# The value projection in rounded fp32r passes, its result copied in quarters by two engines, and halo columns copied in pairs

## What is computed

```python
xn = layernorm(x)                             # (4, 2048, 256)
proj = xn @ in_proj_w + in_proj_b             # (4, 2048, 768)
v = proj[..., :256]
for i in range(2):
    ctrl = proj[..., (i + 1) * 256:(i + 2) * 256]
    h = implicit_filter(...)                  # a filter as long as the sequence
    v = fft_conv(v, h)                        # causal convolution of 2048
    xc = conv3(ctrl, conv_w[i]) + conv_b[i]   # three taps a channel, same padding
    v = v * (xc * sigmoid(xc @ gate_w[i] + gate_b[i]))
out = x + v @ out_proj_w + out_proj_b + ffn(xn)
# ffn: relu(bitlinear(xn, w_fc) + gate * rank-16 term) ** 2 through bitlinear(., w_proj)
```

## Time and profile before

| | us |
|---|---|
| Median of three runs | 860.69 (860.06 to 862.17) |
| Profiled execution, time | 857.83 |
| Profiled execution, span of its instructions | 856.0 |

### The profile page before, as it was taken

The page is one execution under the profiler, slowest core; times in us unless marked ns, Lnnn a source line. Parts: engine busy times, 40 slices in busy tenths (PEclk is TensorE's granted clock), DMA queues, the critical chain, the costliest instruction groups (busy, mean ns, idle before and its releaser), DMA issues.

```text
span 856.0 us, 25946 instructions
## 1 busy us (share of the span) xinstructions
PE 830.3 (97%) x9920; PEld 693.7 (81%) x9921; DVE 617.5 (72%) x1054; ACT 471.6 (55%) x701; POOL 201.0 (23%) x235
## 2 busy tenths in 40 slices
PE   8799999999999998999999999999999999999997
PEld 3588887888888867788888888888888888888997
DVE  7988899889988884555655565556646666567887
ACT  6967777777777854454444444444444444443221
POOL 4944566456645301010101010000000000000000
PEclk9999999999999999999999999999999999999999
DMA  8853432342233278768777868778887877951895
GB/s 224 247 218 115 160 120 98 116 161 115 98 120 140 92 188 227 157 152 194 173 169 154 202 150 202 145 181 182 192 149 182 181 183 132 219 109 49 226 321 195
DMA packets 90544, 142.03 MB, mean 166 GB/s; under 512 B 12846, under 2 KB 70591, under 8 KB 89471
## 3 DMA queue, kind: packets, MB, share of 16 engines
q1 hardware_dynamic: 72846, 101.80, 49.9%
q0 software_dynamic: 7728, 28.05, 10.2%
q10 hardware_dynamic: 9920, 11.54, 4.1%
HBM read 97.39 MB, written 43.97 MB: 165 GB/s over the span
## 4 chain that ended last, share of the span: by engine, by line
PE 51%; DVE 5%; issue 3%; DMA 1%; DVEq 0%; SPq 0%
PE pp L1401 14%; PE py L1420 14%; PE pf L1370 12%; PE pf L1376 3%; PE py L1457 2%; PE py L1388 2%; DVE pp L1169 2%; DMA lead<-filters 1%; DVE GC L1179 1%; DVE xb L1179 1%; PE pp L465 1%; PE pp L467 1%; PE pp L466 1%; PE pf L465 1%; PE pf L467 1%
## 5 line engine op out<-in xcount | busy, mean ns | idle before, releaser
L1300 ACT ACTIVATE r<-pf,fscale 128x512 f32<-128x512 f32 x128 | 88.0, 688 | 124.2 <-PE pf L1376 124.0
L1420 PEld LDWEIGHTS py<-vwin,lead 64*64 64x64 f32 x5120 | 132.7, 132 | 26.8 <-issue 26.8
L1420 PE MATMUL py<-vwin,lead 64*64 64x128 f32 (+4 forms) x5120 | 146.9, 265 | 2.2 <-issue 1.3
L1305 ACT ACTIVATE r_hi<-r 128x512 fp32r<-128x512 f32 x128 | 80.8, 632 | 122.9 <-DVE r L1184 122.9
L1370 PE MATMUL pf<-tokens,split_a 128*128 (+1 forms) x512 | 139.4, 394 | 0.4 <-issue 0.4
L1401 PE MATMUL pp<-wproj,r_hi 128*128 128x256 f32 x512 | 134.6, 296 | 3.8 <-DVE GC L1179 1.8
L1189 DVE TENSOR_TENSOR r_lo<-r,r_hi 128x512 fp32r<-128x512 f32 x128 | 88.2, 689 | 67.2 <-ACT r_hi L1305 67.1
L1401 PE MATMUL pp<-wproj,r_lo 128*128 128x256 f32 x512 | 126.8, 281 | 0.0
L506 POOL TENSOR_SCALAR lead<-lead,norms 128x256 f32<-128x256 f32 x64 | 118.0, 1854 | 3.8 <-POOL norms L500 3.4
L674 DVE SCALAR_TENSOR_TENSOR xc<-ctrl,taps,xc 128x512 f32<-128x512 f32 x128 | 97.7, 783 | 18.5 <-ACT xc L781 17.7
L1401 PEld LDWEIGHTS pp<-wproj,r_hi 128*128 128x128 f32 x512 | 96.2, 188 | 18.3 <-issue 7.4
(11 more groups left out here) (190 smaller groups left out, 1504.9 us busy)
## 6 DMA issues: line engine op xcount, KB each, us to landing
lead<-filters SPq DMA_DIRECT2D x128, 320.0 KB, 6.3
xnT_hbm<-split_b SPq DMA_DIRECT2D x32, 512.0 KB, 3.3
tokens<-xnT_hbm POOLq DMA_DIRECT2D x30, 512.0 KB, 4.9
lead<-in_attn_x SPq DMA_DIRECT2D x16, 512.0 KB, 4.0
gc_hbm<-xc SPq DMA_DIRECT2D x16, 512.0 KB, 2.6
GC<-gc_hbm SPq DMA_DIRECT2D x32, 256.0 KB, 6.6
out<-GC ACTq DMA_DIRECT2D x15, 512.0 KB, 7.2
GC<-in_attn_x POOLq DMA_DIRECT2D x9, 512.0 KB, 7.6
```

Of the source, the lines that this page charges most:

```text
L1300: act.activation(r[j][:, :], pf[:, j, :], ACT.Relu, scale=fscale[:, m:m + 1]).then_inc(relu_done, 1)
L1305: act.activation(r_hi[j][:, :], r[j][:, :], ACT.Copy).then_inc(r_hi_done, 1)
L1420: last = pe.matmul(py[g % 2][q * BW:(q + 1) * BW, side, l, :, A:NB], tile[rows, q * PAIR + l, j * BW:(j + 1) * BW], vwin[g % 2][rows, q, l ...
```

## The change

- V is computed by `split_mm`: the two parts of x, in tiles of 128 tokens, are the stationary operands, and the two parts of Wv (`Wvs`, split once in step -1) the moving ones, 256 columns at a time. That is 4 tiles x 2 halves of the contraction x 3 passes, 24 matmuls a step. Tokens now lie on the partitions without a division by side, so that a copy has to move rows from one half of the partitions to the other for half of the data.
- The bias isn't added there. V is written by four copies of 64 partitions by 512 elements (`to_V`), two of VectorE and two of ScalarE (`store_V`), each writing every second block. In the mixing stage the window copy of order 0 becomes four operations of 128x128 that add the bias.
- xnT is gone with `next_rows`; `next_low` subtracts from pT in PSUM.
- The first x tile's split lies in `xcs[1]` rather than in xn, and `ranks` of the setup stage in GC1.
- Both control buffers lie in one tile `ctrls`, and in a step with both neighbours one VectorE copy of two columns, with a stride between them, fills both halo columns of a channel group.
- SyncE's first loads for the mixing stage wait for the last V rather than for the last controls.

```diff
@@ setup
-            dve.wait_ge(xnT_done, 1)
-            dve.tensor_tensor(xn[1][:, :, :], xnT[:, :, :], xn[0][:, :, :].bitcast(F32), ALU.subtract).then_inc(xn_split, 1)
+            dve.wait_ge(x0_copied, 1)
+            dve.tensor_tensor(xn[1], x0_rows[:, :, :], xn[0].bitcast(F32), ALU.subtract).then_inc(xn_split, 1)
@@ project_stage
-        ctrl = [sb(f"ctrl{i}", [P, 4, CH + 2]) for i in range(2)]
+        WIDE = CH + 2
+        ctrls = sb("ctrls", [P, 2, 4, WIDE])
+        ctrl = [ctrls[:, i, :, :] for i in range(2)]
+        ctrl_flat = ctrls[:, :, :, :].rearrange("p i c t -> p (i c t)")
+        Wv_sides = Wv[:, :, :].rearrange("p k (h s c) -> p k h s c", h=KT, s=SIDES)
+        Wvs_sides = [Wvs[:, part, :, :].rearrange("p k (s h c) -> p k h s c", s=SIDES, h=KT) for part in range(2)]
+        pn_tiles = pn[:, :, :].rearrange("p (t u) c -> p t (u c)", u=SIDES)
+        def split_rows(s0):
+            return xcs[ORDERS - 1] if s0 == 0 else [part[:, :, :] for part in xn]
+        def to_V(copy, eng, s, s0, parity):
+            k = s0 % 4
+            rows = slice(parity * BW, (parity + 1) * BW)
+            for side in (parity, 1 - parity):
+                last = copy(V[side * BW:(side + 1) * BW, :, bass.ds(batch(eng, s, s0), 1), TB * k + parity:TB * k + TB:SIDES].rearrange("p c n a -> p c (n a)"),
+                            pn_tiles[rows, :, side * SLOTS_V:(side + 1) * SLOTS_V].rearrange("p t c -> p c t"))
+            last.then_inc(v_stored, 1)
@@ SyncE
-                    sp.wait_ge(ctrl_mm, 4 * NCH)
+                    sp.wait_ge(v_mm, NCH)
@@ halo
+                    if front and back and k:
+                        lows, highs = ((near, inner_near), (far, inner_far)) if par == 0 else ((far, inner_far), (near, inner_near))
+                        into, step_in = c * WIDE + lows[0], 4 * WIDE + highs[0] - lows[0]
+                        first, step_out = c * WIDE + lows[1], 4 * WIDE + highs[1] - lows[1]
+                        last = dve.tensor_copy(ctrl_flat[:, into:into + step_in + 1:step_in], ctrl_flat[:, first + step_out:first - 1:-step_out])
+                        last.then_inc(halo_done, 1)
+                        return
@@ next_low
-                    if s0:
-                        dve.wait_ge(xnT_done, s + 2)
-                    dve.tensor_tensor(xn[1][:, :, :], xnT[:, :, :] if s0 else pT[:, :, :], xn[0][:, :, :].bitcast(F32), ALU.subtract).then_inc(xn_split, 1)
+                    dve.tensor_tensor(xn[1][:, :, :], pT[:, :, :], xn[0][:, :, :].bitcast(F32), ALU.subtract).then_inc(xn_split, 1)
@@ VectorE, step -1
+                    dve.wait_ge(wv_ready, 1 + KT)
+                    for k in range(KT):
+                        last = dve.tensor_tensor(Wvs_sides[1][:, k], Wv_sides[:, k], Wvs_sides[0][:, k].bitcast(F32), ALU.subtract)
+                    last.then_inc(wv_ready, 1)
@@ VectorE, V
-                    dve.tensor_tensor(V[:, :, bass.ds(batch(dve, s, s0), 1), TB * k:TB * k + TB].rearrange("p c n a -> p c (n a)"),
-                                      pn[:, :, :].rearrange("p i c -> p c i"),
-                                      bv_row[:, :].unsqueeze(2).broadcast_to([P, SLOTS_V, TB]), ALU.add).then_inc(v_stored, 1)
+                    to_V(dve.tensor_copy, dve, s, s0, 0)
@@ ScalarE
-                def next_rows():
-                    act.wait_ge(v_mm, s + 1)
-                    act.wait_ge(xn_split, s + 1)
-                    act.activation(xnT[:, :, :], pT[:, :, :], ACT.Copy).then_inc(xnT_done, 1)
-
                 if s0 < 0:
+                    for k in range(KT):
+                        act.activation(Wvs_sides[0][:, k], Wv_sides[:, k], ACT.Copy).then_inc(wv_ready, 1)
...
                 high(3)
+                def store_V():
+                    act.wait_ge(v_mm, s + 1)
+                    if s0 == 0:
+                        act.wait_ge(stored, 16 * STORES)
+                    to_V(lambda out, rows: act.activation(out, rows, ACT.Copy), act, s, s0, 1)
+                if front and back:
+                    store_V()
                 if back:
                     sigmoid(0)
                     sigmoid(1)
                 if ahead:
                     act.wait_ge(xT_mm, s + 2)
-                    if s0:
-                        next_rows()
-                    act.wait_ge(xn_split, s + 1)
                     act.wait_ge(xn_saved[0], 16 * s + 16)
                     act.activation(xn[0][:, :, :], pT[:, :, :], ACT.Copy).then_inc(xn_hi_done, 1)
-                    if s0 == 0:
-                        act.wait_ge(xn_split, s + 2)
-                        next_rows()
+                if s0 == 0:
+                    store_V()
@@ TensorE
-                    for i in range(TB):
+                    for i in range(TT):
...
                         for k in range(KT):
-                            for side in range(SIDES):
-                                last = pe.matmul(pn[side * BW:(side + 1) * BW, i, :].rearrange("p (h c) -> p h c", h=KT),
-                                                 xnT[:, k, ts], Wv_sides[:, k, :, side, :], start=(k == 0), stop=(k == KT - 1))
+                            last = split_mm(pe, pn_tiles[:, i, :], (x_hi[:, k, ts], x_lo[:, k, ts]),
+                                            (Wvs[:, 0, k, :], Wvs[:, 1, k, :]), k == 0, k == KT - 1)
@@ mix_stage, ScalarE window
+                if order:
+                    act.activation(vwin[g % 2][:, :, :, :, :].rearrange("p b l n a -> p b l (n a)"),
+                                   Vs[:, :, bass.ds(channels(m, g), PAIR), :], ACT.Copy).then_inc(window_done, 1)
+                    return
+                for b in range(SIDES):
+                    for l in range(PAIR):
+                        channel = bass.ds(channels(m, g) + l, 1)
+                        last = act.activation(vwin[g % 2][:, b, l, :, :].rearrange("p n a -> p (n a)"),
+                                              Vs[:, b, channel, :].rearrange("p c x -> p (c x)"), ACT.Identity, bias=bv_slots[:, b, channel])
+                last.then_inc(window_done, 1)
```

More of the change, by code:

```diff
@@ L50, with setup_stage @@
 HALF = PARTS * RANK
-def setup_stage(nc, hbm, ident, bv_row, flag, V, GC1, Wv, Win, Wgate, eps, half, load_x, load_taps, norm, norms, tern, ranks, fscale, stored, weights_stored, xn, xnT, x0, xn_ready, first_done):
+def setup_stage(nc, hbm, ident, bv_row, flag, V, GC1, Wv, Win, Wgate, eps, half, load_x, load_taps, norm, norms, tern, fscale, stored, weights_stored, xn, x0, xn_ready, first_done):
     (in_w, in_b, out_b, freqs, w1, b1, w2, b2, w3, b3, decay, gate_w, fast_b, w_fc, w_proj, u, v, gate,
@@ L369, in _ @@
             act.wait_ge(xT_mm, 1)
-            act.activation(xn[0][:, :, :], x0T, ACT.Copy).then_inc(xn_hi_done, 1)
-            act.activation(xnT[:, :, :], x0T, ACT.Copy).then_inc(xnT_done, 1)
+            act.activation(xn[0], x0T, ACT.Copy).then_inc(xn_hi_done, 1)
+            act.activation(x0_rows[:, :, :], x0T, ACT.Copy).then_inc(x0_copied, 1)
             act.wait_ge(ternT_mm, 1)
@@ L437, in _ @@
             pe.wait_ge(ustack_ready, 1)
-            pe.wait_ge(xnT_done, 1)
+            pe.wait_ge(x0_copied, 1)
             pe.wait_ge(xn_hi_done, 1)
@@ L515, in x_tile, with project_stage @@
     return x.rearrange("n (q i p) d -> (n q) p i d", i=TT, p=P)[bass.ds(c, 1)].rearrange("c p i d -> (c p) i d")
-def project_stage(nc, x, xnT_hbm, gc2_hbm, ident, bv_row, V, GC1, Wv, Win, Wgate, eps, xt, x_loaded, xn_ready, norm, taps, bias_in, gc2_saved, xn, xcs, load_ahead, stored, weights_stored, store_weights, xnT, peaks, flag, first_done, tail):
+def project_stage(nc, x, xnT_hbm, gc2_hbm, ident, bv_row, V, GC1, Wv, Win, Wgate, eps, xt, x_loaded, xn_ready, norm, taps, bias_in, gc2_saved, xn, xcs, load_ahead, stored, weights_stored, store_weights, Wvs, peaks, flag, first_done, tail):
     with ExitStack() as ctx:
@@ L920, in step @@
                     for _ in range(7):
-                        pe.matmul(pT[:, 0, :], ident[:, :], xnT[:, 0, :], start=True, stop=True)
+                        pe.matmul(pT[:, 0, :], ident[:, :], Wvs[:, 0, :, :].bitcast(F32).rearrange("p k c -> p (k c)"), start=True, stop=True)
                 if back:
@@ L1588, in load_taps @@
                     sp.dma_start(taps[:, cs, 5], gate_b[o, :].rearrange("(c p) -> p c", p=P)).then_inc(bias_in, 16)
-            first_done = [weights.enter_context(nc.semaphore(n)) for n in ("xT_mm", "xn_hi_done", "xnT_done", "xn_split")]
-            xnT = weights.enter_context(nc.sbuf_tensor("xnT", [P, KT, CH], F32))
+            first_done = [weights.enter_context(nc.semaphore(n)) for n in ("xT_mm", "xn_hi_done", "wv_ready", "xn_split")]
+            Wvs = weights.enter_context(nc.sbuf_tensor("wv_split", [P, 2, KT, D], F32R))
             peaks = weights.enter_context(nc.sbuf_tensor("peaks", [P, 2, 4], F32))
```

40 lines of the change are left out of this document (20 added, 20 removed).

## The result

The changed kernel takes 863.76 us (median of 8 runs, 861.35 to 865.26) against 860.86 us for the kernel before (8 runs, 858.71 to 862.17): a ratio of 1.0034, 95% interval 1.0018 to 1.0050. The profiled execution of the changed kernel took 863.47 us with a span of 861.8, against 857.83 and 856.0. A gain of 5 us was forecast, and a loss of 3 us came. In the comparisons further down, one of 12 executions of the kernel with the store early and one of 35 of the kernel before took 1131.45 and 1354.8 us, at a mean granted clock of 0.655 and 0.557; the ratios leave these two out (858.31 us is the median of the other 11 with the store early).

What follows compares the result with a forecast made beforehand. GpSimd's normalisation loop was taken to set the 17.06 us step, the VectorE-ScalarE loop next. Thirteen steps gain 4.6 us, step 0 adds 0.5: 5.1 us less, 855.6 us against 860.69; range 852.0 to 861.8.

Steps and rivals of the forecast that it cites:

- The four loops: Projection step: TensorE; GpSimd's normalisation, setting 17.06 us; VectorE with ScalarE, 0.32 us to spare; VectorE alone, about 16.5 us.
- the forecast period of 16.65: Projection stage: new step length of about 16.65 us against 17.06, set by the loop of VectorE with ScalarE.
- V in quarters, ScalarE: Two 64x512 copies ahead of ScalarE's sigmoids, priced at 1.16 us; xn[0] still starts 0.17 us earlier each step.
- The upper bound, 1.36: Highest price given for ScalarE's pair of V copies: twice 0.68 us with no overlap.
- The rival of dear quarters: ScalarE's V copies cost 0.9 us each, the period grows by 0.24 us, total 863.3 us; chance 0.14.
- V in quarters, VectorE: VectorE trades one 1.21 us addition for two 64x512 copies taking 1.27 us: +0.1 us a step.
- Halos: One copy of two columns instead of two copies saves VectorE 0.06 us, four times a step: 0.24 us; bounds 0 and 0.56.
- the break-even price of the pair: ScalarE's two V copies may cost 1.57 us before the period is longer than now.
- xnT: Removing this ScalarE copy between transposes and xn[0] saves 0.92 us, shortening GpSimd's loop from 17.06 to 16.14 us.
- Step 0: First projection step: shorter V lets the controls of step 1 start earlier, 0.5 us gained once.
- Windows: Mixing stage, order 0: four 128x128 bias operations take 1.17 us, +0.55 each window, just covered by ScalarE's idle time.
- Setup and SyncE's loads: Extra Wv split operations are hidden; first mixing loads come some 3 us later, 25 us before use: nothing taken for both.

Runs made afterwards that it cites:

- the kernel with the store early: Changed kernel with ScalarE's two copies of V moved ahead of high(2) and high(3): 858.52 us, ratio 0.9965 to the kernel before.
- the kernel with both moves: Changed kernel with ScalarE's V copies ahead of high(2) and SyncE's first mixing-stage loads split and issued early: 855.05 us, ratio 0.9949 to before; again 856.40, 0.9945.
- the kernel with one window: Changed kernel with one 128x512 window copy in order 0, V's bias left out: 862.88 us, ratio 1.0026 to the kernel before.
- the kernel with the blocks in a row: Changed kernel with V's quarters written as four blocks in a row instead of every second block: 860.77 us, ratio 1.0009 to the kernel before.
- own-half rows: Changed kernel with each quarter of V copied to the partitions it was read from, stride kept: 862.17 us, ratio 1.0018 to the kernel before.

## Why the prediction was wrong, point by point

**The four loops.** That TensorE was not the bound in the steady step was right: saving 0.9 us of it is worth nothing, the wait of about 0.8 us at the gates came (10.7 us in 13 times), and 0.7 us of extra work is free. That the loop of ScalarE and VectorE comes next was right as well, and so was the end of ScalarE's wait for the transposes. But the list was short of the chain that closes over two steps, through TensorE's controls, VectorE's order and GpSimd, 16.77 us a step as read above. No kernel run here has a step under 16.76, so the forecast period of 16.65 was not reached even with the pair off the loop; that it could not have been is not shown.

**V in quarters, ScalarE.** This is the term that failed. The pair was priced at 1.16 us, within 1.13 to 1.36. The sigmoids start 152.59 - 149.89 = 2.70 us after high(2) now, and did so 149.48 - 148.27 = 1.21 us after it, so it added 1.49. From high(2) to xn[0] it was 151.94 - 148.27 = 3.67 and is 153.75 - 149.89 = 3.86: instead of the gain of 0.17 a loss of 0.19, of which 0.06 come back ahead of the subtraction. The remaining 0.13 is close to the step's +0.10. The upper bound, 1.36, failed because I built it from whole durations of single operations. (The middle value wasn't clean either: a pair of 1.22 with a first of 0.68 leaves 0.54 for the second, not 0.57.) It left out that the neighbour ahead, high(3), loses its own overlap, and that a write with a stride of two and from one half to the other has a price. The rival of dear quarters had the right mechanism, and 863.3 us, near the 863.76 measured. That closeness is luck: the loss that it foresaw in the steady steps (3.1 us) was 0.8 to 1.4, and the rest came from elsewhere, the tail above all.

By the Trainium skill ("Advanced Engine Details and Errata", Memory Cachelines) accesses that hit the same line again run at full performance, which for every second float32 I took to mean no penalty. The runs agree on VectorE (685 against 682 ns) and not on ScalarE (633 against 593 ns), where the measurement decides.

**V in quarters, VectorE.** The pair adds 153.29 - 151.85 = 1.44 us where the addition added 1.13: 0.31, not 0.1. With that and without the halo gain the prediction's own figures give 16.5 + 0.31 = 16.8 for VectorE's order, not 16.4, and the 16.79 of the kernel with both moves agrees.

**Halos.** 0.24 us a step were taken, with 0 as the lower bound; the lower bound is what came. The next operation comes as long after the first halo copy, be it one or two (0.12 or 0.18 us). Without it the break-even price of the pair was not 1.57 but 1.16 + 0.17 = 1.33 us, which is inside the bounds that I had given for the price.

**xnT.** The copy is gone, and GpSimd's loop isn't the bound in the changed kernel: the transposes of step 6 end at 151.51 + 1.09 = 152.60, and ScalarE, never idle, comes to xn[0] only at 153.75. The step gained by it what the pair then cost; without it the change would lose some 0.9 us a step more where the pair stands now (argued from the loop, not run).

**Step 0.** 0.5 us were taken, none came in the undisturbed profile of the kernel with one window. I had taken the whole wait of the earlier trace rows for V's; what holds step 1 in its place I didn't follow further.

**Windows.** Right as far as the runs can tell: 1.27 us for four against 1.17, no idle time left in one case of four, and no effect that the times resolve.

**Setup and SyncE's loads.** "I take nothing for both" was the second failed step. I looked at who waits for the loads (the first convolution, 25 us later) and not at who shares the DMA engines with them. The delay itself was forecast well (3 us; 2.9 against the transposes of step 14, and 5.3 on the clock of the profiles, 302.01 - 296.68). But the gated tile is stored 21.6 us after those transposes in both kernels, so it now meets loads that are still under way. In profiles that costs 1.4 to 4.4 us of tail, and in the medians taking it away is worth 3.3 us (863.76 to 860.49), a difference of two medians whose intervals are some 2 us wide each.

**The sum.** Forecast -5.1; measured +2.9. Steady steps +0.8 (1.2 in the profile with one window) instead of -4.6, step 0 nothing instead of -0.5, the tail +1.4 and more instead of 0. How much the tail costs in the mean is not settled: with 3.3 us the terms come to 4.1 to 4.5, with the profile's 1.4 to 2.2 to 2.6. The setup is not in these terms; its clock can add to them.

## What to carry to other kernels

Where several loops are within 0.5 us of each other, price an added operation by the distance between the starts of its neighbours, with its real strides and partitions, and put it into an idle stretch of its engine's order rather than on the loop: here ScalarE's same two copies cost 0.36 us a step less when they stood two lines earlier. List the loops that need two steps to close, too. Of a DMA that moves later, ask what store it will meet, not only when its data are needed.

## What the runs showed of the hardware that I had not expected

- A copy from PSUM to SBUF that moves from one half of the partitions to the other lets the next operation start later: the pair takes 1.37 instead of 1.14 us on ScalarE and 1.42 to 1.44 instead of 1.20 on VectorE, with single durations of 633 and 615 ns, and 685 and 673 ns. The own-half rows still contain the stride of two.
- Writing every second float32 costs ScalarE 633 instead of 593 ns for 64x512, and VectorE 685 instead of 682.
- VectorE's next operation starts 0.12 or 0.18 us after a joined copy of two single columns, the same as after the first of two copies of one column each.
- The granted clock falls to 0.5, the lower of its two levels (1.2 of 2.4 GHz), in some executions and stretches and not in others. At the end of the setup it did so in 7 of 11 profiles of kernels with the changed setup (first transposes at 48.5 to 49.1 us) and not in the other 4 (46.9 to 47.2), nor in the two profiles with the setup of before. Those two are among the least disturbed executions: the mean granted clock is 0.999 in both, and 0.992 to 1.000 in the 91 executions of the kernel before that the ratios use. What decides it, and whether the change makes it more frequent, stays open; no run was made for it. In the tail it followed a stall: in the kernel with the blocks in a row TensorE was busy 1.21 of 4 us, and the next 4 us had 0.50.
